# Gathering attention heads by DMA and keeping the experts' sums feature by token in a one-core transformer block

## What is computed

```
def _L0_attn_ref(x, qw, kw, vw, ow):
    ...
    Q = rope(Q, freq)
    K = rope(K, freq)
    ...
    score = jnp.einsum('bhqd,bhkd->bhqk', Q, K) / scale
    score = score - 10000000000.0 * (1.0 - causal)
    score = score - jnp.max(score, axis=-1, keepdims=True)
    weights = jax.nn.softmax(score, axis=-1)
    attn = jnp.einsum('bhqk,bhkd->bhqd', weights, V)
    merged = jnp.transpose(attn, (0, 2, 1, 3)).reshape(batch, seq, dim)
    return (merged @ ow).astype(x.dtype)
def _L0_ffn_ref(x, router_w, router_b, w1, w3, w2):
    ...
    h = jax.nn.silu(jnp.einsum('td,edf->etf', xf, w1)) * jnp.einsum('td,edf->etf', xf, w3)
    expert_out = jnp.einsum('etf,efd->etd', h, w2)
    out = jnp.einsum('te,etd->td', gates, expert_out)
    return out.reshape(b, s, d)
x = L0_attn_x
x = _layernorm(x + _L0_attn_ref(x, L0_attn_qw, L0_attn_kw, L0_attn_vw, L0_attn_ow), axis=-1)
x = _layernorm(x + _L0_ffn_ref(x, L0_ffn_router_w, L0_ffn_router_b, L0_ffn_w1, L0_ffn_w3, L0_ffn_w2), axis=-1)
```

## Time and profile before

| | before |
|---|---|
| median of 3 runs | 411.76 us (411.66 to 412.97) |
| profiled execution: its time, its span | 413.73 us, 412.0 us |
| PE busy | 386.8 us, 94% |
| PE weight loads (PEld) | 203.3 us, 49% |
| DVE busy | 310.0 us, 75% |
| ACT busy | 260.8 us, 63% |
| POOL busy | 208.2 us, 51% |
| mean granted PE clock | 0.977 of full speed |

### The profile page before, as it was taken

The page is one execution under the profiler, slowest core; times in us unless marked ns, Lnnn a source line. Parts: engine busy times, 40 slices in busy tenths (PEclk is TensorE's granted clock), DMA queues, the critical chain, the costliest instruction groups (busy, mean ns, idle before and its releaser), DMA issues.

```text
span 412.0 us, 7446 instructions
## 1 busy us (share of the span) xinstructions
PE 386.8 (94%) x2402; PEld 203.3 (49%) x2424; DVE 310.0 (75%) x1022; ACT 260.8 (63%) x373; POOL 208.2 (51%) x274
## 2 busy tenths in 40 slices
PE   6897979999999999999999998999999999999992
PEld 2441232323323233232332434888888888888780
DVE  2869799899999999999999761455586568656653
ACT  1361527686866868668686687666566756666560
POOL 7177478542614436044360422756476546755662
PEclk9996889999999999999999999999999999999997
DMA  7474011375232232322310000000000000000000
GB/s 233 160 216 95 0 22 29 88 237 173 55 94 45 47 82 55 95 45 46 85 27 3 3 1 2 0 2 1 2 1 25 2 1 27 2 0 2 25 2 25
DMA packets 46164, 21.14 MB, mean 51 GB/s; under 512 B 30379, under 2 KB 44331, under 8 KB 46126
## 3 DMA queue, kind: packets, MB, share of 16 engines
q1 hardware_dynamic: 42718, 18.44, 17.1%
q10 hardware_dynamic: 3408, 2.23, 1.8%
HBM read 13.11 MB, written 7.35 MB: 50 GB/s over the span
## 4 chain that ended last, share of the span: by engine, by line
PE 80%; DVE 10%; ACT 3%; issue 3%; DMA 2%; POOL 1%; POOLq 0%; SPq 0%; ACTq 0%; DVEq 0%
PE o_bank L1264 16%; PE bank L1338 11%; PE t_bank L1338 11%; PE bank L1223 10%; PE t_bank L1351 10%; PE t_bank L1246 8%; PE small_bank L1223 5%; DVE maxima L960 2%; DVE x_w L956 2%; PE o_bank L1360 2%; PE t_bank L1176 2%; ACT num L766 1%; DVE mg_w L956 1%; DMA wqk<-in_kw 1%; DVE mg_t L956 1%
## 5 line engine op out<-in xcount | busy, mean ns | idle before, releaser
L766 ACT ACTIVATE num<-t_bank 128x1024 f32<-128x1024 f32 (+2 forms) x160 | 141.9, 940 | 65.3 <-PE t_bank L1246 65.2
L659 POOL TENSOR_TENSOR hid_lo<-num,q_op 128x512 fp32r<-128x512 f32 x63 | 81.8, 1302 | 57.7 <-ACT q_op L830 56.5
L621 POOL TENSOR_SCALAR_AFFINE_SELECT num<-num 128x512 f32<-128x512 f32 x64 | 40.2, 638 | 102.2 <-ACT num L766 101.9
L1264 PE MATMUL o_bank<-num,v_op 128*32 128x512 f32 (+3 forms) x768 | 80.1, 497 | 0.1
L1223 PE MATMUL bank<-k_op,q_op 128*128 128x512 bf16 (+7 forms) x241 | 65.3, 327 | 3.4 <-DVE maxima L956 1.3
L830 ACT ACTIVATE q_op<-num 128x512 fp32r<-128x512 f32 x64 | 40.5, 632 | 42.6 <-DVE num L1104 42.1
L960 DVE TENSOR_REDUCE maxima<-bank 128x1 f32<-128x512 f32 x83 | 55.3, 684 | 2.0 <-PE bank L1223 0.8
L1246 PE MATMUL t_bank<-q_op,k_op 64*128 64x512 bf16 (+3 forms) x384 | 49.4, 334 | 3.7 <-ACT num L766 1.3
L1104 DVE TENSOR_TENSOR num<-bank,num 128x512 f32<-128x512 f32 x32 | 22.1, 691 | 34.3 <-ACT num L837 34.0
L1223 PEld LDWEIGHTS bank<-k_op,q_op 128*128 128x128 bf16 x257 | 20.7, 98 | 53.9 <-DVE maxima L960 21.8
L1104 DVE TENSOR_TENSOR num<-t_bank,num 128x512 f32<-128x512 f32 x32 | 22.1, 690 | 26.3 <-ACT num L837 24.0
(11 more groups left out here) (162 smaller groups left out, 654.6 us busy)
## 6 DMA issues: line engine op xcount, KB each, us to landing
q_op<-q_scratch SPq DMA_DIRECT2D x64, 48.0 KB
w_raw<-in_w_all SPq DMA_DIRECT2D x6, 512.0 KB, 4.0
k_op<-k_scratch SPq DMA_DIRECT2D x28, 96.0 KB, 2.2
xT<-in_x_feat SPq DMA_DIRECT2D x4, 256.0 KB, 6.0
x_res<-in_x_tok ACTq DMA_DIRECT2D x4, 256.0 KB, 3.1
q_scratch<-num SPq DMA_DIRECT2D x2, 384.0 KB, 2.8
k_scratch<-num SPq DMA_DIRECT2D x2, 384.0 KB, 2.9
out_tokens<-num SPq DMA_DIRECT2D x3, 256.0 KB, 2.3
```

The source lines that it names most:

```text
L621: pool.affine_select(out=tile, in_=tile, compare_op=ALU.is_ge, fill=0.0, base=0, pattern=[[0, GH], [1, P]], channel_multiplier=-1)\
L659: pool.tensor_tensor(hid_lo[:, m % HB, :], hid[:, m % HB, :], hid_hi[:, m % HB, :].bitcast(F32), ALU.subtract).then_inc(f_lo, 1)
L766: act.activation(num[:, t % PB, :, off:CH].rearrange("p (k i) t -> p i k t", i=2)[:, :, h:h + each, :], t_bank[k % TB][:, :, 0:each * (CH ...
L1264: ins = pe.matmul(o_bank[h * QD:(h + 1) * QD, off:CH], v_op[w][:, kt, h, :], num[:, t % PB, h, off:CH], start=kt == 0, stop=kt == TI * (c ...
```

## The change

1. **Heads.** v_op has 8 columns of ones per head in place of one, so that o_bank holds each head's 8 features and then its sum of weights 8 times. NORM, merged, mg_w and their transposes go. o_sb holds both halves of a group. `gather_heads` sends them by 8 DMAs of 8 rows to o_all (which lies in xT, feature by token) and den_all. It stands on SP behind the send_rows of the next stage's first MROWS, and ACT's OCOPY of half 0 waits for the gather of the group before. In `between`, step 0 is now a reciprocal and a multiplication on DVE, each of 128x512, straight into mg_t.
2. **Experts' sums.** The sum of an expert is multiplied by its gates feature by token (DVE, 128x512) and added to sum_t, which starts from x1_tw (DVE, 128x512). PE transposes once per chunk (L1326 of the new kernel), and the statistics and z read that from PSUM. The gates come as rows: SP stores the chunk's gates to DRAM by 4 DMAs of 4-byte elements and loads them to all partitions by one DMA of 1 MB (`spread_gates`).
3. **Place of `between`.** Step r of the next chunk stands behind the experts' step r + 3 (NEXT_AT), before it stood behind step r + 7.
4. **Prologue.** Loads, warm-up matmuls and the order of the projections are changed, the sums of turns of projections 2 and 3 move from POOL to DVE, and the first loads of k move from ACT's queue to SP's.
5. **Steady and first order.** The strings have no `n`, and some letters stand elsewhere.

```
-STEADY_ORDER = "ssmtttssspssttsspssttsspsstspsttssspmsttsssptsspssttssspssttsspssttsspsnttnpp"
-FIRST_ORDER = "ssssmssssnsssststsstsstsssttsspssttsspmsttssspssttsspssttsspssnttppp"
+STEADY_ORDER = "sstsmtssspsttssspssttssppssttsspmssttsspssttsspssttssspssttsspssttsspsttpp"
+FIRST_ORDER = "ssssmsssssssststsstsstsssttsspssttsspmsttssspssttsspssttsspssttppp"
...
-TR_STEP = Y_STEP = EO_STEP + 1
-STAT_STEP = Y_STEP + UNITS - FT + 1
+TR_STEP = EO_STEP + UNITS - FT + 1
+STAT_STEP = TR_STEP + 1
...
+NEXT_AT = E_LAST
+def next_steps(n, i):
+    r = n - NEXT_AT
+    return [(i + 1 + r // UNITS, r % UNITS)] if i + 1 + r // UNITS < CHUNKS else []
...
+            def gather_heads(n):
+                b, g = divmod(n, NG)
+                sp.wait_ge(o_copied, 1 + NC * (n + 1))
+                for h in range(GH):
+                    for k, dst in enumerate((o_all, den_all)):
+                        at, rows = g * QD + h * DH, h * QD + k * DH
+                        sp.dma_start(dst[at:at + DH, b * S:(b + 1) * S], o_sb[rows:rows + DH, :])\
+                            .then_inc(heads_in[b], 16)
...
                     if step[0] == "MROWS":
                         send_rows(s, step, u if step[1] == 0 else v)
+                        if step[1] == NC - 1 and n > 0:
+                            gather_heads(n - 1)
...
+            def spread_gates(ch):
+                cols = slice(ch * CH, (ch + 1) * CH)
+                sp.wait_ge(c_done, 1 + 2 * ch + 2)
+                for e in range(E):
+                    sp.dma_start(g_dram[e, cols].rearrange("(t p) -> p t", p=P),
+                                 gates[:, ch * TI:(ch + 1) * TI, e:e + 1].rearrange("p t e -> p (t e)"),
+                                 allow_slow_non_contiguous=True)\
+                        .then_inc(g_stored, 16)
+                sp.wait_ge(g_stored, 16 * E * (ch + 1))
+                sp.dma_start(gate_rows[ch % 2][:, :, :], g_dram[:, cols].partition_broadcast(P))\
+                    .then_inc(g_loaded[ch % 2], 16)
...
-                        act.activation(o_sb[c][:, :], o_bank[:, :], ACT.Copy).then_inc(o_copied, 1)
+                        g = n + ahead
+                        if g > 0 and c == 0:
+                            act.wait_ge(heads_in[(g - 1) // NG], 16 * 2 * GH * ((g - 1) % NG + 1))
+                        act.activation(o_sb[:, c * CH:(c + 1) * CH], o_bank[:, :], ACT.Copy).then_inc(o_copied, 1)
...
-                if first and r == 0:
-                    dve.wait_ge(job_read, SB + LAST_JOBS)
-                    dve.wait_ge(c_mgt, 1 + ch)
-                    dve.tensor_copy(mg_w[:, :].rearrange("p (i g r) -> p i g r", i=TI, g=NG),
-                                    merged[:, 1:1 + NG, 0:TI, :].rearrange("p g i r -> p i g r")).then_inc(c_mg, 1)
+                if r == 0:
+                    b, at = ch // NC, slice(ch * CH, (ch + 1) * CH)
+                    dve.wait_ge(heads_in[b], 16 * 2 * GH * NG)
+                    dve.wait_ge(c_y, 1 + ch)
+                    dve.reciprocal(den_all[:, at], den_all[:, at]).then_inc(c_mg, 1)
+                    dve.wait_ge(c_mg, ch + 1)
+                    dve.tensor_tensor(mg_t[:, :], o_all[:, at], den_all[:, at], ALU.mult).then_inc(c_mgs, 1)
...
-                        ins = dve.scalar_tensor_tensor(
-                            y_sb[:, i, :], bank[6 + k][:, i * D:(i + 1) * D],
-                            gates[:, bass.ds(ch * TI + i, 1), e:e + 1].rearrange("p i e -> p (i e)"),
-                            before, ALU.mult, ALU.add)
+                    for k, half in enumerate(halves(ch, e)):
+                        dve.tensor_tensor(gated[:, e % 2, half], bank[4 + e % 2][:, half], gate_rows[ch % 2][:, e, half],
+                                          ALU.mult).then_inc(f_eo, 1)
+                    for k, half in enumerate(halves(ch, e)):
+                        dve.wait_ge(f_eo, 2 + ch * E + e + 1 + k)
+                        if e > 0:
+                            dve.wait_ge(f_y, ch * E + e)
+                        dve.tensor_tensor(sum_t[:, half], gated[:, e % 2, half], (sum_t if e else x1_tw)[:, half],
+                                          ALU.add).then_inc(f_y, 1)
```

More of the change, by code:

```diff
@@ L86 @@
 PROJ_FIRST = 4
-PROJ_AT = (5, 9)
+PROJ_AT = (2, 5, 9)
 V_AT = 3
@@ L510, in _ @@
                     .then_inc(out_stored, 16)
+            for s in range(1, GROUPS + 1):
+                stage(STAGES[s], s, s % 2, load=s < GROUPS - 1)
+            gather_heads(GROUPS - 1)
+            for ch in range(0, CHUNKS):
+                spread_gates(ch)
+                if ch == 0:
+                    continue
+                store_out(ch - 1)
+            store_out(CHUNKS - 1)
             sp.wait_ge(out_stored, 16 * (CHUNKS + 1) + 16)
@@ L675, in _ @@
                 experts(0, n)
+                for step in next_steps(n, 0):
+                    between(*step)
             for i in range(0, CHUNKS - 1):
@@ L680, in _ @@
                     experts(i, n)
-                    between(i + 1, n - HEAD)
+                    for step in next_steps(n, i):
+                        between(*step)
             for n in range(HEAD, Z_STEP + 1):
@@ L932, in _, with stage @@
             third_part(1)
-            for n in range(2, PROJ_FIRST):
-                turns_of(n)
-                if n > 2:
-                    first_rest(n - 1)
-            first_rest(PROJ_FIRST - 1)
-            def stage(plan, s, chain):
+            turns_of(2)
+            sum_of_turns(2)
+            turns_of(3)
+            first_rest(2)
+            sum_of_turns(3)
+            first_rest(3)
+            def stage(plan, s):
                 seen, done = set(), 0
@@ L1137, in experts @@
                     dve.wait_ge(f_rstd, ch + 1)
-                    normalise(lambda i: y_sb[:, i, :], lambda i: z_sb[:, i, :], f_z,
-                              TI // 2 if ch == CHUNKS - 1 else TI)
+                    for k, half in enumerate(halves(ch, E - 1)):
+                        normalise(lambda i: bank[6 + k][:, i * D:(i + 1) * D], lambda i: z_sb[:, i, :], f_z,
+                                  y_mv, y_rstd, range(half.start // P, half.stop // P))
             dve.wait_ge(ld_small, 16 * 6)
             dve.wait_ge(ld_res, 16 * CHUNKS)
-            stage(LAST, GROUPS, last_base)
+            stage(LAST, GROUPS)
             for n in range(E_LAST, HEAD):
                 experts(0, n)
+                for step in next_steps(n, 0):
+                    between(*step)
             for i in range(0, CHUNKS - 1):
@@ L1159, in _ @@
             pe.wait_ge(causal_cleared, 1)
-            for _ in range(WARM):
-                pe.matmul(o_bank[:, 0:CH - QB], causal[:, 0:P], causal[:, 0:CH - QB], start=True, stop=True)
-            for credit in (c_mgt, c_y, c_log, c_x1t):
+            for width in WARM:
+                pe.matmul(o_bank[:, 0:width], causal[:, 0:P], causal[:, 0:width], start=True, stop=True)
+            for credit in (c_y, c_log, c_x1t):
                 pe.sem_inc(credit, 1)
-            pe.wait_ge(rot_ready, 2)
             def project(n):
@@ L1366, in _ @@
             stage(LAST, GROUPS, 0, 0)
+            pe.wait_ge(job_read, SB + NJOBS)
             for n in range(E_LAST, HEAD):
                 experts(0, n)
-            pe.wait_ge(job_read, SB + NJOBS)
+                for step in next_steps(n, 0):
+                    between(*step)
             for i in range(0, CHUNKS - 1):
```

291 lines of the change are left out of this document (102 added, 189 removed).

## The result

| | before | after |
|---|---|---|
| median | 411.76 us (411.66 to 412.97) | 582.54 us (579.76 to 588.55) |
| span of the profiled execution | 412.0 us | 578.0 us |
| PE busy | 386.8 us, 94% | 391.2 us, 68% |
| mean granted PE clock | 0.977 | 0.848 |

The changed kernel takes 1.412 times as long (95% interval 1.405 to 1.418). It is slower by 170.8 us; the prediction was 5.6 us faster, with a range up to 413.0. Medians are over all executions, some of which fall in a slower state; the ratios and their intervals are without those.

A forecast was written before the change was run, and what follows sets the result against it. PE was taken as the bound from the second stage to the end. Gains of 17.7 us less reciprocal terms of 9.9 and 2.2 gave 5.6 us faster: 406.2 us from 411.76, range 396 to 413.

The forecast's parts named there:

- The gates (term 0): Experts: storing and loading the gates' rows takes 12.6 us, hidden behind the wait for the reciprocal; cost 0.
- The rival of late gates: Experts: small elements take 100 ns each, 12.8 us; DVE holds up hid some 7 us in three chunks; 427 us, chance 0.04.
- The gather (term 0): Steady stages: eight issues of 0.43 us bring the heads 7.3 us after the maxima; ACT waits 0.4, PE nothing.
- the rival: Late gather: issues of 0.74 us, heads in after 9.5 us, 10.9 us lost over the stages; 417 us, chance 0.13.
- the turning point of 0.63: Gather: issue time in us from which the late-gather rival decides, at 0.8 us lost a stage.
- The room: Steady stages: ACT's copy of half 0 can come 1.0 us late before PE has to wait.
- The reciprocal: Each 128x512 reciprocal on DVE takes 3.6 us; PE waits for it in chunks 1 to 3, 9.9 us, and LAST, 2.2.
- The dearer: Rival: a reciprocal of 512 elements per partition takes 4.4 us on DVE; 409.4 us, chance 0.10.
- the cheap rival: Rival: a reciprocal of 512 elements per partition takes 0.78 us on DVE; 396.8 us, chance 0.27.
- What PE loses: Transposes leave PE: 9.3 us in attention (1.1 a steady stage), 6.9 us in the experts.
- The prologue (1.5 us): Prologue: sums moved from POOL to DVE and better-placed loads gain 1.5 us, with 0 and 3 as ends.
- the gains alone: Whole kernel: transposes in attention 9.3, in the experts 6.9 and the prologue 1.5 us, together 17.7 us faster.

The follow-up runs named there:

- b1: a1_no_store with o_sb twice, by turns, so ACT's copy of half 0 waits for the gather of two groups before; 434.7 us.
- c1: Changed kernel, whole computation, with gates stored as 512-byte rows and loaded by expert, o_sb twice and reciprocals moved; 425.4 us, 1.032 of the kernel before.
- b4: a1_no_store with o_sb twice, without the four reciprocals, and with the next chunk behind step r + 7 again; 418.6 us, 1.014 of the kernel before.
- d2: c1 with the residual left in PSUM, where DVE's statistics and x1_w read it; 421.6 us, 1.021 of the kernel before.
- e2: e1 with the residual left in PSUM; 412.9 us, 0.9995 of the kernel before.
- e1: Heads' half of the change alone on c1's attention, with the heads' multiplication moved from step 0 and the fourth reciprocal piece behind step 16; 414.8 us, 1.003.
- a1_no_store: The changed kernel without the four stores of the gates, the load reading four rows of an input (wrong numbers); 452.9 us, 1.094 of the kernel before.
- a4: Changed kernel with the gates in one store of 512 elements of 16 bytes, the load reading the input (wrong numbers); 453.7 us.

## Why the prediction was wrong

- **The gates (term 0): the step that failed first, 129.6 of the 170.8 us.** The step "at the mean of a packet, 26 ns, on 16 engines, they take 3.4" took the time of the packets for the time until the store is counted as done. The packets themselves were about as short as assumed (21 ns on average), but the count came 31.4 us after the last issue, nine times the 3.4; with the elements apart from each other it comes after 3.5. The rival of late gates had the right mechanism with 12.8 us and a chance of 0.04. It also had three chunks; all four waited. The load, estimated at 5.8 us, landed in 9.3 to 10.7, for 1 MB.
- **The gather (term 0): failed by its issue.** The step "the gather's are plain, so I take 0.43" rested on a form with two dimensions; the DMAs of 8 rows take 0.67 from one to the next. The heads are in 9.4 us after the maxima (132.63 to 142.05), as the rival had it (9.5, with 0.74), and over the turning point of 0.63 that it named. The room was too large as well: ACT waits 2.35 us and PE 2.06, so 0.3 us of room and not 1.0. Cost by b1: 18.2 us, where the rival had 10.9. ACT wanted the copy 7.1 us after the maxima (142.05 less 2.35), close to the 6.9 estimated: that part held.
- **The reciprocal: right in its duration, its term a third too high.** 3.34 us against 3.6 (6.25 ns an element, by the pieces of 128 at 943 ns in c1: (3342 - 943) / 384). PE's waits for mg_t were 3.2 us in chunk 1 and 1.8 in chunks 2 and 3, 6.8 in all, and 1.6 in LAST; taking the reciprocals away gave 8.5 us where the terms were 9.9 + 2.2. In LAST it was not the maxima, as the prediction had it, but mg_t that PE waited for. The dearer and the cheap rival are out.
- **What PE loses: right in the attention, not seen in the experts.** The stages became 1.10 us shorter where nothing waits. In the experts the transposes are gone (L1326 stands once a chunk), but PE's busy time in b4's chunk is 0.8 us less where the prediction had 1.7, and no run showed a chunk shorter than 37.8 us.
- **The prologue (1.5 us): about right, as far as one trace of the kernel before can say.** PE's second and fourth matmul of the maxima stand at 52.70 and 77.11; they stood at 54.02 and 78.29, 1.3 and 1.2 us later. But in the traces of b1 and b4, whose prologue is the same, the fourth stands at 77.92 and at 75.08, so a gain of this size is not clear of the scatter.
- **Left out: DVE beside POOL.** Even without stores, late gather, reciprocals and the new place (b4), the kernel stands 23 us above what the gains alone would give. Against 36.1 us for a chunk (37.8 less 1.7), its two chunks are 5.7 and 7.4 us longer, and 4.8 us of each is PE standing for work of DVE and ACT. Of such waits, runs showed those behind instructions held beside POOL (x1_w 3.8 us by d2 and 1.9 by e2, the multiplication within the 5.9 of e1). The bound was taken as "PE, as long as the others don't hold it up", and an amount of work for DVE was priced by free durations. The mean clock is no part of it (0.979 in b4, 0.977 before), though the second of b4's chunks ran at 0.96 where 1.00 was before; in a1_no_store it is (0.946). How the rest of the 23 us divides was not settled.

The two failed steps have one form: a transfer was priced by a row of something else (packets for completions, an issue of another shape), and its position just inside the room was taken for hidden.

## What to carry to other kernels

A store of 4-byte elements next to each other in DRAM can take several times what the records of its packets say; before such a path is put between two engines, turn the data so that it leaves in larger pieces (here rows of 512 bytes by one PE transpose, 1.2 us in place of 31.4; a4's 16-byte elements needed no transpose and 2.4 us, but a load from that layout was not tried). A DMA that must land before an engine's next copy needs a second buffer rather than an estimate of its issue time: with o_sb twice, 18 us went. Where PE is the bound at 100%, taking matmuls away by giving DVE work asks first where DVE's instructions will stand: here the loss shrank when they read PSUM, or started where POOL was idle, and nobody waited for them in the same step, and even then no gain was left that could be measured.
